# Fused cross-attention and feed-forward kernel: where the gammas are multiplied, and which engine normalises for the feed-forward half

## The reference, cut to what matters

```python
# x, ctx: (64, 64, 128) float32; 16 heads of 8; feed-forward width 512
def rms_norm(t, gamma):                       # over the 8 elements of a head
    return t * rsqrt(mean(t * t) + EPS) * gamma
q = layernorm(x) @ Wq.T + bq
k, v = split(ctx @ Wkv.T + bkv)               # k at the even columns, v at the odd ones
q, k = rms_norm(q, q_gamma), rms_norm(k, k_gamma)
x = x + softmax(q @ k.T / sqrt(8)) @ v        # per batch row and head
h = fix(layernorm(x) @ w1 + b1)               # fix: round to multiples of 1/256
x = x + fix(fix(gelu_piecewise_linear(h)) @ w2 + b2)
```

## Time and profile before

| | |
|---|---|
| three runs | 208.56, 209.04, 210.41 us |
| profiled execution, its own time | 210.93 us |
| its span, first to last instruction | 209.1 us |
| busy: PE, PEld, DVE, ACT, POOL | 184.6, 141.1, 186.9, 148.2, 117.8 us |
| granted TensorE clock, mean | 0.982 |
| chain that ended last, by engine | PE 46%, DVE 22%, POOL 13%, issue 12%, DMA 3% |
| transfers | 7.97 MB, 38 GB/s on average |

### The profile page before, as it was taken

One profiled execution on the slowest core, in us unless ns is written; L12 is line 12 of the kernel. 1 busy time (PEld: TensorE's weight loads), 2 busy tenths in 40 slices (PEclk: granted clock), 3 DMA queues, 4 the chain that ended last, 5 costly groups with the idle time before them and its releaser, 6 DMA issues.

```text
span 209.1 us, 8050 instructions
## 1 busy us (share of the span) xinstructions
PE 184.6 (88%) x3324; PEld 141.1 (67%) x3324; DVE 186.9 (89%) x348; ACT 148.2 (71%) x228; POOL 117.8 (56%) x164
## 2 busy tenths in 40 slices
PE   6857899899999999999899799869899999984693
PEld 2446788688888887888788546356567666553692
DVE  6978998979999998989899777999999999999882
ACT  5134787687777887689677779967878888878411
POOL 7537557766768677686664501474444565644530
PEclk9999999999999999999999999999999999999679
DMA  3363111011101111011000000000101101010103
GB/s 90 109 192 85 55 53 36 22 53 53 55 19 41 53 55 53 6 28 31 3 3 3 3 5 3 0 0 0 53 6 45 50 0 53 0 50 0 50 3 100
DMA packets 14836, 7.97 MB, mean 38 GB/s; under 512 B 1072, under 2 KB 14576, under 8 KB 14800
## 3 DMA queue, kind: packets, MB, share of 16 engines
q1 hardware_dynamic: 14272, 7.20, 12.2%
q10 hardware_dynamic: 528, 0.25, 0.4%
HBM read 5.35 MB, written 2.10 MB: 36 GB/s over the span
## 4 chain that ended last, share of the span: by engine, by line
PE 46%; DVE 22%; POOL 13%; issue 12%; DMA 3%; SPq 1%; ACT 1%; DVEq 0%; POOLq 0%
POOL y_raw L398 8%; PE bank_o L1047 8%; PE banks_p L1017 8%; PE banks_p L985 6%; PE banks_s L1031 5%; DVE frac L834 5%; DVE banks_p L841 4%; PE banks_p L999 4%; PE bank_o L1057 4%; DVE y_raw L849 3%; PE banks_p L981 3%; DVE act_q L855 2%; DMA c_in<-in_ctx_dram 2%; PE banks_p L951 2%; DVE seg L828 2%
## 5 line engine op out<-in xcount | busy, mean ns | idle before, releaser
L398 POOL TENSOR_TENSOR y_raw<-g_lo,y_raw 128x1024 f32<-128x1024 f32 x15 | 35.5, 2364 | 34.2 <-DVE frac L834 33.2
L455 ACT ACTIVATE probs<-banks_s 128x512 f32<-128x512 f32 x64 | 33.0, 609 | 1.3 <-PE banks_s L1031 1.3
L1169 PEld LDWEIGHTS bank_o<-w,act_q 128*128 128x128 f32 x224 | 28.8, 205 | 7.2 <-DVE act_q L855 7.0
L1169 PE MATMUL bank_o<-w,act_q 128*128 128x128 f32 x224 | 30.4, 293 | 1.8 <-DVE act_q L855 1.5
L334 POOL TENSOR_TENSOR parts<-qk_hat,parts 128x512 f16<-128x512 f32 x16 | 18.6, 1161 | 22.3 <-DVE parts L630 22.3
L1154 PE MATMUL banks_s<-x2T,w 128*128 128x512 f32 x60 | 30.6, 592 | 0.0
L516 ACT ACTIVATE g_lo<-seg,gelu_lo 128x1024 f32<-128x1024 f32 x16 | 18.4, 1150 | 8.4 <-DVE seg L828 8.4
L525 ACT ACTIVATE banks_p<-seg,gelu_hi 128x1024 f32<-128x1024 f32 x16 | 17.9, 1118 | 6.8 <-DVE y_raw L849 6.8
L1017 PE MATMUL banks_p<-ident,parts 128*128 128x128 f16 x256 | 19.6, 219 | 2.2 <-POOL parts L334 1.8
L1047 PE MATMUL bank_o<-probs,v_blk 128*32 128x64 f32 x1024 | 20.7, 222 | 0.0
L849 DVE SCALAR_TENSOR_TENSOR y_raw<-banks_p,frac 128x1024 f32<-128x1024 f32 x16 | 19.6, 1224 | 0.6
(11 more groups left out here) (115 smaller groups left out, 426.6 us busy)
## 6 DMA issues: line engine op xcount, KB each, us to landing
x_all<-in_x_dram SPq DMA_DIRECT2D x16, 128.0 KB, 2.6
c_in<-in_ctx_dram SPq DMA_DIRECT2D x16, 128.0 KB, 2.2
out_dram<-x_all SPq DMA_DIRECT2D x7, 256.0 KB, 2.3
w<-in_L_ffn_w_dram SPq DMA_DIRECT2D x2, 256.0 KB, 3.2
out_dram<-x_all SPq DMA_DIRECT2D x2, 128.0 KB, 1.9
b_rows<-in_L_ffn_b_dram SPq DMA_DIRECT2D x1, 192.0 KB, 3.5
wkv_raw<-in_L_xattn_Wkv_dram ACTq DMA_DIRECT2D x1, 128.0 KB, 2.9
bkv_rep<-in_L_xattn_bkv_dram SPq DMA_DIRECT2D x1, 128.0 KB, 4.5
```

Source lines behind the costliest of these rows:

```text
L398: g.tensor_tensor(y_raw[u][:], g_lo[n % 3][:], y_raw[u][:], ALU.add).then_inc(S[f"gelu{u}_done"], 1)
L455: a.activation(probs[i][:].rearrange("p t g n -> p (t g n)"), bank_s(i), ACT.Exp).then_inc(S["probs_ready"], 1)
L1169: last = t_.matmul(out, act_q[u][:, c, P * t:P * t + P], w2[:, CH // UNITS * u + c, :], start=False, stop=(u == UNITS - 1 and t == GT - 1 ...
```

## The change

- The second q projection and its bias are gone on TensorE (L969, L981); `bank_qk` now gets q without the gammas, and so does the square on ScalarE, which reads one bank instead of a strided pair. The folded weights `wqgT`, the folded bias row and their set-up instructions are gone.
- VectorE multiplies `gqk` onto the normalised q (`scale_q`, 128x256, in place) between the normalisation and the high parts, which now wait for it.
- The layer norm for the feed-forward half moves, for steps 0 to 12, from VectorE to ScalarE as `Identity(x * rstd + bias)`, two instructions of 128x128 between the exponential of `rms` and the copy of the attention output, in the turn s+3 instead of s+2. GpSimd makes the bias, minus mean times rstd, with two more instructions on 128x2 after the inverse deviation. Steps 13 to 15 stay on VectorE.
- TensorE's projection of v and the transposes of the inputs no longer wait for the squares.

The core of the diff:

```diff
@@ GpSimd, rstd_x2(s)
                 g.tensor_tensor(rstd2[:], var_eps2[:], minus_half[:], ALU.pow).then_inc(S["ln2_rstd"], 1)
+                if s < STEPS - 3:
+                    pool.wait_ge(S["ln2_rstd"], s + 1)
+                    g.tensor_tensor(shift2[:], stats2[:, :, 1], rstd2[:], ALU.mult).then_inc(S["ln2_shift"], 1)
+                    pool.wait_ge(S["ln2_shift"], s + 1)
+                    g.tensor_tensor(bias2[:], zeros[:], shift2[:], ALU.subtract).then_inc(S["ln2_bias"], 1)
@@ ScalarE
-                a.activation(qk_sq[:].rearrange("p w t d -> p w (t d)"),
-                             banks_p[:, 256:1280].rearrange("p (w r) -> p w r", w=2)[:, :, 0:2 * DIM], ACT.Square).then_inc(S["qk_squared"], 1)
+                a.activation(qk_sq[:].rearrange("p w t d -> p (w t d)"), bank_qk, ACT.Square).then_inc(S["qk_squared"], 1)
+            def norm_x2(s):
+                wait(act, "ln2_bias", s + 1)
+                for t in range(2):
+                    a.activation(xn2_all[:, tok(s, t, 2)], x_all[:, tok(s, t, 2)], ACT.Identity, bias=bias2[:, t:t + 1],
+                                 scale=rstd2[:, t:t + 1]).then_inc(S["xn2_ready"], 1)
@@ ScalarE, step(s): after rms(s + 1), before copy_outT(s - 1)
+                if runs(s - 3, STEPS):
+                    norm_x2(s - 3)
@@ ScalarE, after the loop: copy_parts(last), copy_x2(1)
+            norm_x2(last - 3)
             copy_outT(last - 1)
@@ VectorE
             def ln2_statistics(s):
                 wait(dve, "x1_ready", s + 1)
-                wait(dve, "xn2_ready", 2 * s)
+                if s <= STEPS - 3:
+                    wait(dve, "ln2_bias", s)
+                else:
+                    wait(dve, "xn2_ready", 2 * s)
+            def scale_q(s):
+                wait(dve, "qk_normed", s + 1)
+                q = qk_hat[:, 0, :, :].rearrange("p t (h d) -> p (t h) d", d=DH)
+                v.tensor_tensor(q, q, gqk[:].unsqueeze(1).to_broadcast([P, 2 * HEADS, DH]), ALU.mult).then_inc(S["q_scaled"], 1)
@@ VectorE, highs(s)
-                wait(dve, "qk_normed", s + 1)
+                wait(dve, "q_scaled", s + 1)
@@ VectorE, step(s)
                     normalise(s + 1)
+                    scale_q(s + 1)
                     highs(s + 1)
                 if runs(s - 1, STEPS):
                     heads_out(s - 1)
-                if runs(s - 2, STEPS):
-                    norm_x2(s - 2)
@@ TensorE
-                wait(pe, "qk_squared", s)              # transpose_in
-                if not first:
-                    bias_q()                           # project_qk
-                for t in range(2):
-                    t_.matmul(bank_in[:, DIM * (2 + t):DIM * (3 + t)], xcT[:, 0, t, :], wqT[:], start=(first and t == 0), stop=(t == 1 and not first))
-                    for which, w in ((0, wqgT[:]), (1, wkT[:].rearrange("p h d -> p (h d)"))):
+                    for which, w in ((0, wqT[:]), (1, wkT[:].rearrange("p h d -> p (h d)"))):
-                wait(pe, "qk_squared", s + 1)          # project_v
```

More of the change, by code:

```diff
@@ L115, in xattn_ffn @@
         w2 = sb("w2", [P, CH, DIM])
-        B_Q, B_QG, B_K, B_1, B_2, B_END = 0, DIM, 2 * DIM, 3 * DIM, 3 * DIM + FF, 4 * DIM + FF
+        B_Q, B_K, B_1, B_2, B_END = 0, DIM, 2 * DIM, 2 * DIM + FF, 3 * DIM + FF
         BR = 96
@@ L121, in xattn_ffn @@
         b_rest = sb("b_rest", [BR, B_END])
-        b_parts = sb("b_parts", [P, B_END], F16)
+        b_parts = sb("b_parts", [P, B_END + DIM], F16)
         x_all = sb("x_all", [P, TOKENS])
@@ L134, in xattn_ffn @@
         rstd2 = sb("rstd2", [P, 2])
+        shift2 = sb("shift2", [P, 2])
+        bias2 = sb("bias2", [P, 2])
+        zeros = sb("zeros", [P, 2])
         xn2_all = sb("xn2_all", [P, TOKENS])
@@ L202, in xattn_ffn @@
             bound_sq_ready g_done g_loaded g_stats g_moments g_var g_rstd g_centred g_xn g_in_t g_in_copied
-            g_qk g_squared g_ms g_logged g_rms g_normed  g_high g_parts_t g_parts_copied g_scores g_max
-            ln2_stats ln2_var ln2_rstd xn2_ready x2_t x2_t_copied h_first hz_first h_proj hz_ready
+            g_qk g_squared g_ms g_logged g_rms g_normed g_scaled  g_high g_parts_t g_parts_copied g_scores g_max
+            ln2_stats ln2_var ln2_rstd ln2_shift ln2_bias xn2_ready x2_t x2_t_copied h_first hz_first h_proj hz_ready
             seg_ready frac_ready glo_ready ghi_ready rise_ready slope_done gelu0_done gelu1_done actq0_ready actq1_ready
@@ L303, in _ @@
             g.memset(minus_half[:], -0.5).then_inc(S["consts_set"], 1)
-            pool.wait_ge(S["consts_set"], 2)
+            g.memset(zeros[:], 0.0).then_inc(S["consts_set"], 1)
+            pool.wait_ge(S["consts_set"], 3)
             def layer_norm(out, x, mean, spread, times, n, sems, count):
@@ L766, in guard @@
                 dve.wait_ge(S["g_normed"], t + 1)
+                v.tensor_tensor(hat[:, 0:HEADS, :], hat[:, 0:HEADS, :], gqk[:].unsqueeze(1).to_broadcast([P, HEADS, DH]),
+                                ALU.mult).then_inc(S["g_scaled"], 1)
+                dve.wait_ge(S["g_scaled"], t + 1)
                 for which in range(2):
@@ L963, in bias_qk @@
                 def bias_qk():
-                    t_.matmul(bank_qk.rearrange("p (w t d) -> p w t d", w=2, t=2), pick16[:],
-                              b_parts[:, B_QG:B_1].rearrange("p (w d) -> p w d", w=2).unsqueeze(2).to_broadcast([P, 2, 2, DIM]),
+                    return t_.matmul(bank_qk.rearrange("p (w t d) -> p w t d", w=2, t=2), pick16[:],
+                              b_parts[:, B_Q:B_1].rearrange("p (w d) -> p w d", w=2).unsqueeze(2).to_broadcast([P, 2, 2, DIM]),
                               start=not first, stop=first)
[L968 to L974, removed]
+                if not first:
                     wait(pe, "qk_normed", s)
@@ L987, in project_qk @@
                     pe.wait_ge(S["bqk_ready"], 1)
-                    bias_qk()
-                    last = bias_q()
+                    last = bias_qk()
                 last.then_inc(S["qk_proj"], 1)
@@ L1084, in weights_ready @@
                 pe.wait_ge(S["wq_ready"], 2)
-                pe.wait_ge(S["w_ready"], 9)
+                pe.wait_ge(S["w_ready"], 8)
                 pe.wait_ge(S["bqk_ready"], 1)
@@ L1096, in guard @@
                 weights_ready()
-                bias(bank_qk[:, 0:2 * DIM], B_QG, 2 * DIM, 1)
+                bias(bank_qk[:, 0:2 * DIM], B_Q, 2 * DIM, 1)
                 pe.wait_ge(S["g_in_copied"], t + 1)
-                bias(bank_in[:, 2 * DIM:3 * DIM], B_Q, DIM, 1)
-                t_.matmul(bank_in[:, 2 * DIM:3 * DIM], xcT[:, 0, 0, :], wqT[:], start=False, stop=True)
-                t_.matmul(bank_qk[:, 0:DIM], xcT[:, 0, 0, :], wqgT[:], start=False, stop=False)
+                t_.matmul(bank_qk[:, 0:DIM], xcT[:, 0, 0, :], wqT[:], start=False, stop=False)
                 t_.matmul(bank_qk[:, DIM:2 * DIM], xcT[:, 1, 0, :], wkT[:].rearrange("p h d -> p (h d)"),
```

11 lines of the change are left out of this document (2 added, 9 removed).

## The result

The changed kernel takes 215.13 us (median of 4 runs, 214.25 to 215.80) against 209.08 (4 runs, 208.56 to 210.41): ratio 1.0271, interval 1.0218 to 1.0323. Slower, as forecast, and 0.1 us from the predicted time. The profiled execution has a span of 213.0 us and a time of 215.07. In each of the executions on record, of whichever kernel, the time is 1.7 to 2.1 us more than the span.

What follows compares the result with a forecast made beforehand. The prediction took a loop through TensorE, VectorE and GpSimd to set the 6.41 us step. Multiply +6.9, contention +1.4 and absorbed lateness -2.3 gave +6.0 us on the median 209.04: 215.0 us, range 210.5 to 219.

Steps and rivals of the forecast that it cites:

- The loop: Each attention step: a round from TensorE through VectorE and GpSimd back to TensorE, whose links sum to the 6.41 us step.
- The predicted signs: In the new profile: steps of 6.85 to 7.0 us, TensorE waiting about 1 us for GpSimd, VectorE idle before L649.
- TensorE's 0.56 us: Removing the second q projection and its bias from each step on TensorE; costed at nothing, giving only slack.
- VectorE's L606: Feed-forward layer norm, 1.29 us of VectorE's queue per step, outside the loop; taking it off was predicted to gain nothing.
- `scale_q` at 0.46: New VectorE multiply inside the loop: 0.46 us more in each of 15 steps, +6.9 us.
- two at 0.48 each: The moved layer norm's two ScalarE instructions, some 0.87 us together, fitting 0.82 us of idle time; costed at nothing.
- Contention: GpSimd's small instructions colliding with VectorE's multiply or cast: 0.1 us a step, +1.4 us; bounds 0 and 0.58 a step.
- Absorbed lateness: TensorE's late steps, 2.6 us in excess of 13 equal steps, nearly all absorbed by its new slack: -2.3 us.
- Start and end: Start-up and feed-forward half of the run: no change, at most 0.1 us.
- Rival A: Faster: the full engines set the step, which becomes the longest queue; 205 or 200.6 us, chance 0.09.
- Rival B: No change: the loop's hand-overs are not rigid and shrink by 0.3 us together; 209 us, chance 0.08.
- Rival C: Slower by more: GpSimd and VectorE hold each other up every step, if ScalarE's norm ends late; 218.5 to 221.8, chance 0.13.

Runs made afterwards that it cites:

- experiment 4: The changed kernel with its feed-forward layer norm back on VectorE, so the multiply alone remains: 214.93 us, ratio 1.0255.
- experiment 1: The changed kernel with the `scale_q` multiply left out: 210.45 us, ratio 1.0021; in a second series 209.26 us, ratio 1.0011.
- experiment 5: The kernel before with only the feed-forward layer norm moved to ScalarE, q still projected twice: 209.35 us, ratio 1.0009.
- experiment 11: The kernel before with the second q projection and its bias left out, no `scale_q`, norm still on VectorE: 208.86 us, ratio 0.9992.
- experiment 2: The changed kernel with the multiply issued behind the high parts, writing a tile that nobody reads: 211.93 us, ratio 1.0113.
- experiment 6: The changed kernel with high and low parts made for k first, then the multiply, then those for q: 215.68 us, ratio 1.0288.
- experiment 3: The kernel before, unchanged, profiled again: 208.72 us, ratio 0.9972; its profiled execution took 209.30 us with a span of 207.5.
- experiment 9: The kernel before with the feed-forward norm on ScalarE and the low parts made by VectorE instead of GpSimd: 207.88 us, ratio 0.9964.
- experiment 8: The changed kernel with the low parts made by VectorE instead of GpSimd: 211.63 us, ratio 1.0136.
- experiment 10: The changed kernel with low parts on VectorE and the feed-forward layer norm on GpSimd instead of ScalarE: 212.48 us, ratio 1.0170.

## Why the prediction was right

- **The loop sets the step: shown.** With the multiply in it 6.85 to 6.86 (experiment 4), without it 6.40 (experiments 1, 5, 11), with it elsewhere 6.60 (experiment 2). The predicted signs are all there: 0.46 between L619 and L630, TensorE waiting for POOL by 0.85 to 1.16 us in nine of the thirteen steps, VectorE idle, 92 us from step 15 on.
- **TensorE's 0.56 us and VectorE's L606 worth nothing: shown,** by experiments 11 and 5, each within 0.1% of the kernel before. The reading of the earlier trace rows, a step with VectorE idle that is no shorter, had said so of L606. Of TensorE's 0.56 it could not, since TensorE was full in that step as well: only the sum of the links spoke for it until experiment 11.
- **`scale_q` at 0.46, 15 times: +6.9.** Measured 0.455, so +6.8. The row of the same shape in another stage was the right price to the nanosecond (424 and 425).
- **ScalarE:** two at 0.48 each, 0.86 together, as worked out, in a hole of 0.82 us: L457 stands 0.9 behind L463's start, and nothing comes later.
- **Contention: +1.4 was too much.** It is 0 here: in an undisturbed step the small instructions end 0.75 us ahead of the low parts. The bound of 0 was the right one. In experiments 2 and 6 it is 0.20 and 0.35 us, when a long instruction of one engine overlaps one of the other. The prediction says that the change moves the collision of L606 into the loop; L606 did collide, at its own cost, off the loop: a pair takes 1.29 us there and 0.59 where GpSimd is idle, behind the last step of the kernel before:

```profile
119.99 0.59 DVE L606 TENSOR_SCALAR xn_all<-x_all,stats,rstd 128x128 f32<-128x128 f32 x2
```

- **Absorbed lateness: -2.3 was too much,** for a reason that the prediction could have seen: it noted that its execution lay 1.9 above the median, and yet took all of that execution's late steps as usual ones. It had put the 1.9 outside the span, where they were not, and so took the late steps of a long execution off a median that did not contain them. Experiment 3 has 1.25 of them. That the slack absorbs such steps is seen in the changed kernel's own execution: it has three pauses in the score matmuls, 1.0 us in all, and its 89.15 us are 13 x 6.86 with nothing over. Against the long execution the figure is -2.77.
- **Start and end:** -0.1, where I had 0: against experiment 3, -0.3 up to step 2 and +0.2 from step 15 on.

The sum as measured is 6.8 - 1.25 - 0.1 = +5.45 us, and the spans of experiment 3 and of the changed kernel are 5.5 apart. The medians are 6.05 apart (5.7 by the ratio); the last 0.6 lies within the spread of the executions (before: 207.8 to 210.9 in most runs). The forecast's +6.0 contained two errors of opposite sign, +1.4 and -1.05, that nearly cancel. The nearness to the time is thus partly luck; the sign, the step of 6.85 and its cause are not.

Rival A failed on its premise: the engines were full, but did not set the step; TensorE's list stood 0.11 us under the loop (6.29 in experiment 9). Rival B failed, since no link shrank when TensorE and VectorE got idle time. Rival C's condition, a `norm_x2` on ScalarE that ends late, came about in one step of the changed kernel (that of 66.17, which is no longer than the others), without a cost; in experiment 1 it cost 0.2 us in a late step.

## What to carry to other kernels

When two engines look full, follow the first instruction of a step back to itself through its releasers, and add up the links. If they make the step without a remainder, only what stands in that round counts: 1.3 us off VectorE and 0.56 off TensorE bought nothing, and 0.42 us put into the round cost 0.46 fifteen times. Before moving work out of such a round, look at what it will then run beside, and what the engine that receives it will then be full of: in experiment 8 the step stopped at 6.4 us, where VectorE's own list stood.

Take lateness that "will be absorbed" from more than one profiled execution.

## What the runs showed of the hardware

- A VectorE multiply with two SBUF inputs (0.42 us) lengthened a GpSimd subtract on 128x512 from 1.16 to 1.36 us; a VectorE cast to fp16 that started while a GpSimd subtract was under way took 0.78 to 0.93 instead of 0.43 us (experiments 2 and 6).
- GpSimd's `tensor_scalar` on 128x128 with two operands per partition took 0.79 to 1.40 us, 1.25 in the median, beside VectorE's work (experiment 10). VectorE's took 0.34 where GpSimd was idle and 0.64 beside GpSimd's subtract and addition (kernel before, L606).
- Pauses of 0.2 to 0.9 us in TensorE's score matmuls (1.3 once, in experiment 10), with nothing in the profile as their cause, differ in number from one execution of the same program to the next: three and one in the kernel before, five and one in experiment 1's.
- In the changed kernel the granted clock was 0.50 from 22 to 24 us, the lower level, with TensorE busy for 1.87 of the 2.00 us; in the kernel before it was 1.00 there, with 1.70 busy. Yet step 1 began only 0.35 us later than before, less than the 0.46 of its multiply.
